# A fused graph attention and residual normalisation kernel: the next scores move behind the last projection, their transpose behind the second residual's statistics

## The reference

```python
u = h @ h.T / sqrt(384)
p = softmax(u, axis=-1)
delta = p * adj
attn = delta / (delta.sum(axis=2, keepdims=True) + 1e-10)
h_left, h_self, h_right = (h @ W.T + b for W, b in the three pairs)
ctx = attn_above_diagonal @ h_left + diag(attn)[:, None] * h_self + attn_below_diagonal @ h_right
o = relu(layernorm(ctx, eps=1e-12) * gamma + beta)
out = layernorm(h + o, eps=1e-5)
```

## Time and profile before

| | before |
|---|---|
| median of 3 runs | 458.7 us (458.45 to 459.05) |
| profiled execution | 458.62 us, span 456.9 us |
| mean granted TensorE clock | 0.995 of full speed |
| TensorE busy | 448.2 us, 98% of the span |
| VectorE busy | 387.2 us, 85% |
| ScalarE busy | 324.3 us, 71% |
| POOL busy | 210.0 us, 46% |

### The profile page before, as it was taken

The page is one execution under the profiler, slowest core; times in us unless marked ns, Lnnn a source line. Parts: engine busy times, 40 slices in busy tenths (PEclk is TensorE's granted clock), DMA queues, the critical chain, the costliest instruction groups (busy, mean ns, idle before and its releaser), DMA issues.

```text
span 456.9 us, 9729 instructions
## 1 busy us (share of the span) xinstructions
PE 448.2 (98%) x2637; PEld 445.9 (98%) x2637; DVE 387.2 (85%) x1367; ACT 324.3 (71%) x717; POOL 210.0 (46%) x295
## 2 busy tenths in 40 slices
PE   9999999999999999999999999999999999999993
PEld 8999999999999999999999999999999999999992
DVE  6977988888889887989788988888988888987876
ACT  5856677677678677677677677677677677676764
POOL 1144345553345553345654345553346553345542
PEclk9999999999999999999999999999999999999997
DMA  7765455676355575455566555566555666454312
GB/s 233 252 223 168 130 178 185 192 208 196 130 182 195 184 206 181 149 177 195 183 194 198 152 173 189 184 204 188 154 171 182 191 203 186 148 174 150 106 60 103
DMA packets 84227, 80.60 MB, mean 176 GB/s; under 512 B 7148, under 2 KB 76528, under 8 KB 84208
## 3 DMA queue, kind: packets, MB, share of 16 engines
q1 hardware_dynamic: 84144, 80.38, 55.5%
q0 software_dynamic: 64, 0.01, 0.0%
HBM read 52.04 MB, written 28.31 MB: 176 GB/s over the span
## 4 chain that ended last, share of the span: by engine, by line
issue 29%; POOL 20%; PE 14%; DVE 13%; ACT 10%; DMA 6%; SPq 5%; POOLq 0%; DVEq 0%; ACTq 0%
PE ps_proj L507 7%; POOL scaled L1141 7%; DMA dt_raw<-dt_dram 6%; POOL shifted L1145 6%; SPq L332 4%; ACT normed L653 4%; POOL rstd L1135 4%; DVE y_sb L900 3%; ACT ps_scores L605 3%; DVE proj_lo L856 3%; POOL dt_right L1129 2%; DVE delta L825 2%; PE ps_ctx L541 2%; DVE cross_turned L792 2%; ACT dt_full L637 2%
## 5 line engine op out<-in xcount | busy, mean ns | idle before, releaser
L507 PE MATMUL ps_proj<-w_hi,xt_split 128*128 128x384 f32 x1128 | 236.1, 334 | 0.0
L507 PEld LDWEIGHTS ps_proj<-w_hi,xt_split 128*128 128x128 f32 x1128 | 199.1, 188 | 0.0
L507 PE MATMUL ps_proj<-w_lo,xt_split 128*128 128x384 f32 x564 | 128.0, 334 | 0.0
L1135 POOL TENSOR_TENSOR rstd<-var_eps,minus_half 128x4 f32<-128x4 f32 x31 | 34.2, 1102 | 184.1 <-DVE var_eps L886 184.1
L507 PEld LDWEIGHTS ps_proj<-w_lo,xt_split 128*128 128x128 f32 x564 | 100.5, 188 | 0.0
L623 ACT ACTIVATE ps_proj<-bias 128x384 f32<-128x384 f32 x188 | 90.4, 494 | 1.8 <-DVE proj_lo L856 1.6
L1141 POOL TENSOR_TENSOR scaled<-normed,gamma_sb 128x384 f32<-128x384 f32 x60 | 61.5, 1025 | 31.0 <-ACT normed L653 31.0
L627 ACT ACTIVATE proj_hi<-ps_proj 128x384 fp32r<-128x384 f32 x128 | 63.5, 497 | 14.1 <-PE ps_proj L507 12.9
L647 ACT ACTIVATE ps_ctx<-ps_proj,diag 128x384 f32<-128x384 f32 x64 | 35.6, 556 | 49.1 <-PE ps_proj L507 49.1
L856 DVE TENSOR_TENSOR proj_lo<-ps_proj,proj_hi 128x384 fp32r<-128x384 f32 x128 | 67.3, 544 | 1.4 <-ACT proj_hi L627 1.4
L1145 POOL TENSOR_TENSOR shifted<-scaled,beta_sb 128x384 f32<-128x384 f32 x61 | 62.4, 1022 | 2.5
(11 more groups left out here) (113 smaller groups left out, 678.4 us busy)
## 6 DMA issues: line engine op xcount, KB each, us to landing
x_sb<-in_x SPq DMA_DIRECT2D x32, 384.0 KB, 4.4
xt_sb<-in_x_t SPq DMA_DIRECT2D x31, 384.0 KB, 3.8
out_dram<-out_sb SPq DMA_DIRECT2D x31, 384.0 KB, 2.9
adj_sb<-in_adj SPq DMA_DIRECT2D x32, 256.0 KB, 4.4
dt_dram<-turned SPq DMA_DIRECT2D x31, 256.0 KB, 2.0
dt_raw<-dt_dram SPq DMA_DIRECT2D x124, 64.0 KB, 2.0
cross_dram<-cross_turned SPq DMA_DIRECT2D x29, 256.0 KB, 2.0
cross_raw<-cross_dram SPq DMA_DIRECT2D x116, 64.0 KB, 2.0
```

The source lines that it names most:

```text
L507: mm = nc.tensor.matmul(ps_proj[bank(at, g)][:, 0:H], halves[c][half], moving[w][:, c, :], start=False, stop=True, skip_group_check=True)
L1135: nc.gpsimd.tensor_tensor(rstd[at.slot(2)][:], var_eps[:], minus_half[:], ALU.pow).then_inc(rstd_ready, 1)
```

## The change

TensorE's order: `cross(ahead)` stood between the groups 4 and 5 of the projections. It now stands behind group 5, ahead of the contexts. VectorE's order: `turn_cross(ahead)` stood behind the residual and statistics of row tile 0. It now stands behind those of row tile 1. This is so in batch 1, which has a written-out order of its own, and in all later ones. Nothing else is edited.

```diff
@@ tensor: one(at)
-                    if g == 4 and ahead.exists(BATCHES):
+                    if i == NG - 1 and ahead.exists(BATCHES):
                         cross(ahead)
@@ vector: one(at)
                     residual(before, 0)
                     residual_stats(before, 0)
                     split_proj(at, 3)
-                    turn_cross(ahead)
                 else:
...
                     split_proj(at, 3)
                     residual(before, 0)
                     residual_stats(before, 0)
-                    if ahead.exists(BATCHES):
-                        turn_cross(ahead)
                 residual(before, 1)
                 residual_stats(before, 1)
+                if ahead.exists(BATCHES):
+                    turn_cross(ahead)
                 if nxt.exists(BATCHES):
                     diagonal(nxt)
```

## The result

| | before | after |
|---|---|---|
| median | 458.59 us (457.96 to 459.05, 6 runs) | 482.44 us (480.13 to 484.59, 6 runs) |
| ratio | | 1.0526, 95% interval 1.0508 to 1.0545 |
| profiled execution | 458.62 us, span 456.9 | 483.74 us, span 482.0 |
| cross transposes, first to last | 34.9 to 420.4, 28 periods of 13.77 | 37.5 to 446.1, 28 periods of 14.59 |

The change makes the kernel 5.3% slower. The forecast was 477.5 us in a range of 471 to 486.

The account below looks back on a forecast made before the run. TensorE (13.71 us per batch) bounds the kernel; the change makes the ring decide at 5.28 + 8.11 + 1.03 = 14.42 us. First transpose 36.9, 28 periods 403.8, tail 35.1, plus 1.7: 477.5 us, range 471 to 486.

Parts of the forecast that it names:

- a second ring: Cross transpose, SyncE's store and dt_raw loads, ScalarE's split, VectorE to the next transpose: 13.39 us against TensorE's 13.71.
- TensorE's exchange of two groups: Score products (1.23 us) and group 5 (1.56 us) change places on TensorE: no cost, one 0.3 us wait goes.
- 1.03 us more in the ring: Second residual and its statistics now precede VectorE's cross transpose, so store and dt_raw loads go out 1.03 us later.
- The leg: From the cross transpose through SyncE's store, dt_raw loads and ScalarE's split to VectorE's L866: stays 5.28 us.
- The stalls of the shift: VectorE's 0.91 us waits for POOL's power should vanish, the power ending at 4.92 us, before L866 at 5.28.
- Rival C: VectorE's stalls for POOL's power stay: 14.80 us per batch, 488.1 us; chance 0.05.
- The second residual does not meet POOL: On VectorE it starts 0.93 us after POOL's last instruction and takes 0.52 us, with 1.14 as the other end.
- D: POOL slides 0.93 us or more against VectorE and the second residual takes 1.14 us: 494.9 us; chance 0.03.
- TensorE is held ahead of group 4: TensorE idles 0.71 us per batch at L507, waiting for ScalarE's seed, in 28 batches.
- Rival A: The move is hidden and TensorE stays the bound at 13.71 us: 456.6 or 458.6 us; chance 0.06.
- Rival B: Half is hidden: leg shortened to about 4.9 us by less transfer traffic, period 14.0, 466 us; chance 0.04.
- tail: Span behind the last cross transpose: 35.1 us, 1.4 us shorter because group 5 is reached sooner.

Follow-up runs that it names:

- more_stats: Kernel before, old order, with two more VectorE statistics instructions right ahead of the cross transpose from batch 2 on: 474.18 us, ratio 1.0355.
- three_loads: Changed kernel with three instead of four dt_raw loads from batch 2 on: 463.15 us, 1.0117 times the kernel before.
- pe_only: Kernel before with only TensorE's order changed, cross(ahead) behind group 5: 458.44 us, ratio 1.0008.
- after_queue: Changed kernel with SyncE's dt_raw loads put ahead of the cross store: 462.77 us, 1.0100 times the kernel before.
- earlier: Kernel before with the cross transpose between the first residual and its statistics from batch 2 on: 458.13 us, ratio 1.0000.
- few_loads: Changed kernel with the loads of x and adj cut to 32 columns of one row tile from batch 4 on: 479.85 us, 1.0471 times the kernel before.
- dve_only: Changed kernel with TensorE's old order restored, so only VectorE's order differs from the kernel before: 478.51 us, ratio 1.0435.

## Why the prediction was right

The direction and the mechanism held. The time, 482.44 us, lies in the range, 4.9 us above the forecast. By its own steps:

- **TensorE is full, and a second ring is 0.32 us shorter.** Shown by more_stats and three_loads, which lengthen and shorten the ring on two different engines and move the time with it.
- **TensorE's exchange of two groups costs nothing.** Shown by pe_only, where the ring has slack. With VectorE's change the kernels with and without the exchange are 4 us apart, and why stays open.
- **1.03 us more in the ring.** Measured 9.06 - 8.17 = 0.89 in the medians, where the 8.17 holds stalls for POOL's power. Against the 20 batches of before in which neither POOL's power nor cross_raw held VectorE for 0.3 us (7.98 to 8.30, median 8.11) it is 0.95. The pair itself took 1.06 us (241.57 to 242.63), and the way from L866 to the first residual became 0.17 us shorter (median 6.54 to 6.37), where the working had allowed about 0.1.
- **The leg stays.** 5.33 beside 5.35. The forecast had 5.28 for it, 0.05 too little, and 8.11 + 1.03 = 9.14 for the rest, 0.08 too much. That the working let two such terms cancel was a choice without a sum behind it, and in part luck. VectorE's shorter work in it was won for nothing: L866 waits 1.49 us instead of 0.43.
- **The stalls of the shift go.** From 5.9 us in 9 waits to 0.6 us in one. Rival C is thereby refuted.
- **The second residual does not meet POOL.** It took 0.54 or 0.55 us in all 28 batches, and D is refuted with it. POOL ended 0.92 us before it began; 0.93 was forecast. The first residual, which does meet POOL's addition, has a median of 1.12 us.
- **TensorE is held ahead of group 4, 0.71 us per batch.** The sum is near (28 x 0.71 = 19.9; 23.3 us of weight loads waiting), but in 47 waits and not 28: group 5's seed also holds it. The working had 0.05 us there; in the batch above the weight loads waited 0.45 us ahead of group 4 and 0.42 ahead of group 5.
- **Rival A**, the move hidden, falls with after_queue: the slack was not in the ring. **Rival B**, a shorter leg, falls with the leg of 5.33.
- **Two slips that did not matter.** The 0.06 us per batch over TensorE's 13.71 were put down to stalls for POOL's power. They did not slow the kernel: over before's 28 periods TensorE was busy 385.2 of 385.5 us. The first transpose merely comes early in before (34.9, beside 36.1 in pe_only, and the last at 420.4 beside 420.1), so rival A's gain was not there to be had, as `earlier` shows too. And the lower end of the range names 2 us for the first transpose but adds 1; with 2 it is 470.

What the sum missed is 6.2 us of span (475.8 beside 482.0):

| term | forecast | measured | difference |
|---|---|---|---|
| first transpose | 36.90 | 37.55 | +0.65 |
| 28 periods | 403.8 | 408.6 | +4.8 |
| tail | 35.1 | 35.9 | +0.8 |

The periods are the mis-sized term. The typical one was right (14.42 against a median of 14.41), but I had put every batch at a typical value, and a ring without slack hands most of each late landing on. Three of 28 periods, 15.48, 16.36 and 15.91, exceed 14.4 by 4.6 us together. The longest holds this row, VectorE waiting for cross_raw in the changed kernel:

```profile
104.91 0.42 DVE L808 TENSOR_TENSOR cross_raw<-cross_raw,ps_scores 128x256 f32<-128x256 f32 x1 [2.23 <-DMA cross_raw<-cross_dram]
```

The kernel before has such delays too: its trace has legs of 6.53 and 6.22 us and a wait of 1.59 us for cross_raw, in three batches of 14.2 to 14.6 us. But the batches behind the first two took 13.4 and 13.3 us, and TensorE's idle time stayed at those 0.3 us: the slack absorbed them. Its runs lie within 1.1 us of each other, those of the changed kernel within 4.5.

## What to carry to other kernels

A profile with one engine at 98% can hold a second ring through other engines and queues that is nearly as long; look for an instruction that waits for the same transfer in every batch with a dependent right behind it, and add up the ring before moving anything in it. The wait is only the sign, the sum decides: in pe_only that wait was twice as long and cost nothing. One engine that issues its DMAs in order ties together transfers that have nothing to do with each other: here a store that waited on SyncE also held the loads behind it, so moving an instruction late on VectorE moved another tensor's loads. Once a ring is the bound, the size of the loss needs the late transfers too, not only the typical batch; here they added a fifth of it.

## What the runs showed of the hardware

TensorE's clock fell behind some waits, and not behind others of nearly the same length. The first three rows are waits in the changed kernel, the fourth is one in few_loads (line numbers 3 higher):

```profile
63.36 0.79 PE L507 MATMUL ps_proj<-w_hi,xt_split 128*128 128x384 f32 x3 [1.54 <-ACT ps_proj L623]
...
108.12 0.80 PE L507 MATMUL ps_proj<-w_hi,xt_split 128*128 128x384 f32 x3 [1.96 <-ACT ps_proj L623]
...
439.90 0.82 PE L507 MATMUL ps_proj<-w_hi,xt_split 128*128 128x384 f32 x3 [1.81 <-ACT ps_proj L623]
...
437.04 0.79 PE L510 MATMUL ps_proj<-w_hi,xt_split 128*128 128x384 f32 x3 [1.84 <-ACT ps_proj L626]
```

The windows of the changed kernel give the granted clock (the column behind POOL's). From 110 to 112 us, in the long batch when TensorE was busy again, it is 0.50 of full speed, that is 1.2 GHz:

```profile
108.00:110.00 2.00, 1.88 (x9) 1.88 (x10) 1.88 (x8) 1.34 (x4) 0.46 (x1) 0.86 0.02 6
110.00:112.00 2.00, 2.00 (x9) 2.00 (x9) 1.93 (x5) 2.00 (x5) 0.00 (x0) 0.50 0.33 125
112.00:114.00 2.00, 2.00 (x11) 2.00 (x11) 1.53 (x10) 1.75 (x4) 0.00 (x0) 0.79 0.00 0
```

It fell again behind the wait of 1.81 us (0.52 from 442 to 444), but not behind that of 1.54 us (1.00 throughout), nor in few_loads behind that of 1.84 us (1.00 throughout). So the length of a wait alone does not tell whether the clock falls. In the long batch the cross transpose then waited 0.5 us for the slow products, so a late transfer was made a little later still by the clock.

In dve_only the clock fell too, behind a wait of 1.95 us that ended at 63.38 us:

```profile
64.00:66.00 2.00, 2.00 (x9) 2.00 (x9) 1.97 (x5) 1.54 (x3) 0.00 (x0) 0.55 0.34 131
66.00:68.00 2.00, 2.00 (x9) 2.00 (x9) 1.97 (x8) 0.19 (x1) 0.00 (x0) 0.60 0.00 0
```

The period that began at 66.92 us took 15.48 us there: VectorE waited 1.3 us for the contexts and then 0.91 us for POOL's power. So neither of the two orders of TensorE keeps its clock from falling.

The Trainium skill, "TensorE: Matmul & The Clock Gate", part 1, says that the clock gate has two states, 1.2 and 2.4 GHz. The rows agree with it: in windows of a quarter microsecond the clock is 1.00 from 109.00 to 109.25 us and 0.50 from 109.50 to 110.00, and values between, as 0.86 and 0.79, are of windows in which it changed.
